# Two slots of edge attributes on one load of stationary columns, and digit tables made in fewer steps, in a graph network on one core

## What is computed

```python
def sage_conv(x, src, dst, W_l, b_l, W_r, n_nodes):
    agg = jax.ops.segment_sum(x[src], dst, num_segments=n_nodes)
    cnt = jax.ops.segment_sum(jnp.ones((src.shape[0], 1), x.dtype), dst, num_segments=n_nodes)
    return (agg / jnp.maximum(cnt, 1.0)) @ W_l.T + b_l + x @ W_r.T
def _mp_layer(x, src_f, dst_f, ea_f, W, b):
    m = jnp.concatenate([x[dst_f], x[src_f], ea_f], axis=1) @ W.T + b
    return jax.nn.relu(jax.ops.segment_sum(m, dst_f, num_segments=n))
x = _layernorm(x + _L0_gnn_ref(x, edge_index, ...), axis=-1)
x = _layernorm(x + _L1_gnn_ref(x, src, dst, edge_attr_16, ...), axis=-1)
```

## Time and profile before

| | us |
|---|---|
| median of 3 runs | 1181.01 (1178.44 to 1189.15) |
| the profiled execution | 1185.87 |
| its span from first to last instruction | 1184.0 |
| TensorE / VectorE / ScalarE busy over the span | 1054.0 / 711.7 / 368.8 |
| mean granted TensorE clock, share of full | 0.933 |

### The profile page before, as it was taken

One profiled execution on the slowest core, in us unless ns is written; L12 is line 12 of the kernel. 1 busy time (PEld: TensorE's weight loads), 2 busy tenths in 40 slices (PEclk: granted clock), 3 DMA queues, 4 the chain that ended last, 5 costly groups with the idle time before them and its releaser, 6 DMA issues. The chain is left out here.

```text
span 1184.0 us, 21105 instructions
## 1 busy us (share of the span) xinstructions
PE 1054.0 (89%) x8433; PEld 656.5 (55%) x8433; DVE 711.7 (60%) x1415; ACT 368.8 (31%) x733; POOL 104.9 (9%) x125
## 2 busy tenths in 40 slices
PE   0259999999999997999999999996899998899993
PEld 0258888899999984445555444443344444344441
DVE  5698979899899852623434755444555654233434
ACT  2475667686776530200000011113310105100000
POOL 4121212232211110000000000000000000000001
PEclk9968888899898897999999999998899998899997
DMA  6325535646455448963875436745036745037740
GB/s 160 48 69 196 187 112 204 201 135 234 126 173 170 120 171 254 404 257 127 311 277 219 164 118 267 290 150 218 14 122 240 289 179 218 18 122 270 287 181 22
DMA packets 67310, 216.89 MB, mean 183 GB/s; under 512 B 32176, under 2 KB 45227, under 8 KB 53667
## 3 DMA queue, kind: packets, MB, share of 16 engines
q1 hardware_dynamic: 59188, 164.51, 39.2%
q0 software_dynamic: 8016, 50.95, 12.0%
HBM read 170.68 MB, written 44.74 MB: 182 GB/s over the span
## 5 line engine op out<-in xcount | busy, mean ns | idle before, releaser
L1325 PE MATMUL PM<-Aring,Xop 128*128 128x512 fp8e4 (+1 forms) x1960 | 398.5, 363 | 0.0
L1325 PEld LDWEIGHTS PM<-Aring,Xop 128*128 128x128 f16 x1960 | 181.6, 98 | 216.6 <-issue 16.3
L1848 ACT ACTIVATE F<-PH,bag 64x512 f32<-64x512 f32 (+1 forms) x39 | 25.4, 657 | 382.4 <-PE PH L1544 382.3
L1325 PE MATMUL PM<-Ares,Xop 128*128 128x512 fp8e4 x588 | 137.0, 387 | 2.2 <-ACT Xop L1887 1.4
L772 PE MATMUL PW<-Aring 128*128 128x52 fp8e4 (+3 forms) x2151 | 115.9, 217 | 19.6 <-ACT F L836 17.6
L772 PEld LDWEIGHTS PW<-Aring 128*128 128x128 fp8e4 x2151 | 111.6, 103 | 22.8 <-ACT F L836 19.2
L785 PE MATMUL PA<-Ares,ea 128*128 128x32 f16 x1867 | 112.3, 235 | 0.0
L1681 DVE TENSOR_SCALAR S<-PM 128x256 f32<-128x256 f32 (+1 forms) x75 | 31.4, 418 | 130.6 <-PE PM L1325 118.8
L785 PEld LDWEIGHTS PA<-Ares,ea 128*128 128x128 f16 x1867 | 108.5, 116 | 0.0
L1325 PEld LDWEIGHTS PM<-Ares,Xop 128*128 128x128 f16 x588 | 55.9, 99 | 72.7 <-issue 10.0
L836 ACT ACTIVATE F<-PW 128x392 uint16<-128x392 f32 x196 | 85.4, 510 | 7.7 <-PE PW L772 5.4
(11 more groups left out here) (154 smaller groups left out, 1121.1 us busy)
## 6 DMA issues: line engine op xcount, KB each, us to landing
Aring<-adj SPq DMA_DIRECT2D x72, 1568.0 KB, 9.8
adj<-Aring POOLq DMA_DIRECT2D x12, 1568.0 KB, 6.1
adj<-Xop POOLq DMA_DIRECT2D x12, 1568.0 KB, 6.3
Ares<-adj SPq DMA_DIRECT2D x6, 1568.0 KB, 22.0
rc<-ea_sum SPq DMA_DIRECT2D x36, 128.0 KB, 5.8
eaf<-in_erow SPq DMA_DIRECT2D x62, 51.0 KB
Aring<-adj SPq DMA_DIRECT2D x4, 784.0 KB, 4.3
rc<-rc_d SPq DMA_DIRECT2D x12, 256.0 KB, 10.6
```

What stands on the lines that cost most here:

```text
L1325: last = nc.tensor.matmul(o, x[:, h, :], rhs, start=h == 0, stop=h == NT - 1)
L1848: nc.scalar.activation(F[0:64, c:c + w], PH[b % 2][0:64, 0:w], ACT.Relu, bias=t["bag"][:, 4 + conv:5 + conv]).then_inc(s_hr, 1)
```

## The change

- **Attribute slots in pairs.** The operand `ea16` is laid out in groups of two slots, 80 columns apart: slot 0 has columns 0 to 31, slot 1 columns 32 to 63, column 64 is the ones. `ohd` holds the two slots' one-hot columns interleaved. One matmul loads the columns of both slots and moves 64 columns for both, or 32 where only one of the two belongs to the window (`steps()` lists them). Of each product half is used; `sums` reads the even columns from partitions 0 to 31 and 64, the odd ones from 32 to 63 and 64, into `eas` and the new `odd`, with four copies for one; gpsimd adds the two before it stores the sum.
- **Low parts.** `eax` goes. ScalarE's `high(c)` is one copy; VectorE subtracts in place in `eaf` and raises `s_rest`; a new `low(c)` on ScalarE scales the remainder into `ea16` and raises `s_lo`. It stands behind `table` in ScalarE's round.
- **Digit tables.** `B` is made with its value in it by a bitwise and of patterns, in place of a comparison and a product (`valued`); the last value is half and doubled by a factor per partition in `evacuate` (`level`). `D` and its product become one scalar_tensor_tensor of 128 elements per value. `digits` has three more small tensor_tensor instructions.

```diff
@@ -164,9 +164,11 @@
 PD = 32
 NPW = NP // PD
+PJ[-1] += sum(PJ) % 2
+GW = 80
...
+def steps():
...
-        D = within(1, [128, 4, 128], u16)
-        Bv = within(2, [128, 8, 128], u16)
-        ohd = within(2, [128, 4, PD, CH], f16)
+        ohd = within(2, [128, 4, CH // 2, PD, 2], f16)
-        eax = sb("eax", [128, 2, CH, 16])
-        ea_flat = sb("ea16", [128, 4, CH * 33 + 95], f16)
-        ea16 = ea_flat[:, :, 0:CH * 33].rearrange("p g (k c) -> p g k c", c=33)
+        odd = sb("odd", [33, 2, SW])
+        ea_flat = sb("ea16", [128, 4, CH // 2 * GW + 48], f16)
+
+        def part(r, n, at):
+
+            x = ea_flat[:, r, 0:n // 2 * GW].rearrange("p (g k) -> p g k", k=GW)[:, :, 0:64]
+            return x.rearrange("p g (s c) -> p g s c", c=32)[:, :, :, at:at + 16]
...
@@ -535,6 +580,9 @@
                     for st in sums_after(h - 1):
                         n = SW if st < NST - 1 else LASTW
                         g.wait_ge(s_eas, st + 1)
+                        nc.gpsimd.tensor_tensor(eas[:, st % 2, 0:n], eas[:, st % 2, 0:n], odd[:, st % 2, 0:n],
+                                                ALU.add).then_inc(s_add, 1)
+                        g.wait_ge(s_add, st + 1)
                         g.dma_start(m["ea_sum"][:, st * SW:st * SW + n], eas[:, st % 2, 0:n]).then_inc(s_eo[st % 2], 16)
@@ -577,28 +625,29 @@
                 node, src, d = vs[:, t % 2, 0, :], vs[:, t % 2, 1, :], dig[:]
                 op = nc.vector.tensor_scalar
-                op(d[:, 1], src, 0x0E, None, ALU.bitwise_and)
+                op(d[:, 1], src, 4, 8, ALU.logical_shift_right, ALU.bitwise_and)
-                op(d[:, 5], node, 6, 0x40, ALU.logical_shift_left, ALU.bitwise_and)
-                op(d[:, 6], src, 3, 8, ALU.logical_shift_left, ALU.bitwise_and)
-                op(d[:, 7], src, 4, 8, ALU.logical_shift_right, ALU.bitwise_and).then_inc(s_dig, 1)
+                op(d[:, 5], src, 1, 7, ALU.logical_shift_right, ALU.bitwise_and)
+                op(d[:, 6], node, 6, 0x40, ALU.logical_shift_left, ALU.bitwise_and)
+                op(d[:, 7], src, 3, 8, ALU.logical_shift_left, ALU.bitwise_and).then_inc(s_dig, 1)
                 v.wait_ge(s_dig, 2 * t + 1)
-                tt = nc.vector.tensor_tensor
-                own(tt(d[:, 4:6], d[:, 4:6], base[:], ALU.bitwise_or))
-                tt(d[:, 4:6], d[:, 4:6], d[:, 6:8], ALU.logical_shift_left).then_inc(s_dig, 1)
-
-            def onehot(to, n, first_, table):
+                tt, u = nc.vector.tensor_tensor, d.bitcast(u16)
+                wait = tick(tt(d[:, 4], d[:, 4], d[:, 6], ALU.bitwise_or))
+                over = tick(tt(d[:, 5], d[:, 5], d[:, 7], ALU.bitwise_or))
+                v.wait_ge(s_own, wait)
+                own(tt(d[:, 4], d[:, 4], base[:, 0], ALU.bitwise_or))
+                v.wait_ge(s_own, over)
+                tt(u[:, 5], one[:], u[:, 5], ALU.logical_shift_left)
+                tt(u[:, 4], u[:, 4], u[:, 1], ALU.logical_shift_left).then_inc(s_dig, 1)
+
+            def onehot(to, n, first_, table, how=ALU.is_equal):
...
-                    table.rearrange("p (o g s) -> p o g s", o=1, s=16).broadcast_to(shape), ALU.is_equal)
-
-            def valued(to, of, n, table):
-                return nc.vector.tensor_tensor(
-                    to, of, table.bitcast(u16).rearrange("p (o s) -> p o s", o=1).broadcast_to([128, n, 128]), ALU.mult)
+                    table.rearrange("p (o g s) -> p o g s", o=1, s=16).broadcast_to(shape), how)
...
                 d, w = dig[:], wide(t)
-                onehot(B[:], 8, 8, d[:, 1])
-                wait = tick(onehot(D[:, 0:w], w, 42, d[:, 3]))
+                onehot(B[:].bitcast(i16), 8, 8, d[:, 5], ALU.bitwise_and)
                 onehot(A[:], 8, 0, d[:, 0])
+                for i in range(w):
+                    nc.vector.scalar_tensor_tensor(Dv[:, t % 2, i, :], d[:, 3], 4.0 * i, d[:, 4], ALU.is_equal, ALU.mult)
                 shape = [128, HS, 26, 2]
                 nc.vector.tensor_tensor(
                     H[:, t % 2], iv[:].rearrange("p v (o e) -> p o v e", o=1).broadcast_to(shape),
-                    d[:, 2].rearrange("p (q o e) -> p q o e", o=1, e=2).broadcast_to(shape), ALU.is_equal)
-                v.wait_ge(s_own, wait)
-                valued(Bv[:], B[:], 8, d[:, 4])
-                valued(Dv[:, t % 2, 0:w], D[:, 0:w], w, d[:, 5]).then_inc(s_sm, 1)
+                    d[:, 2].rearrange("p (q o e) -> p q o e", o=1, e=2).broadcast_to(shape),
+                    ALU.is_equal).then_inc(s_sm, 1)
@@ -662,17 +710,16 @@
                     v.wait_ge(s_pp, c - 3)
                 own(nc.vector.tensor_tensor(vd[:, c % 2, 0:n], eaf[:, c % 3, 0:n, 16].bitcast(i32),
                                             pb[:, c * CH:c * CH + n], ALU.subtract))
-                shape = [128, PD, CH // 2, 2]
+                shape = [128, CH // 2, PD, 2]
                 nc.vector.tensor_tensor(
-                    ohd[:, r].rearrange("p d (q e) -> p d q e", e=2),
-                    iop[:].rearrange("p d (o e) -> p d o e", o=1).broadcast_to(shape),
-                    vd[:, c % 2].rearrange("p (o q e) -> p o q e", o=1, e=2).broadcast_to(shape), ALU.is_equal)
+                    ohd[:, r], iop[:].rearrange("p d (o e) -> p o d e", o=1).broadcast_to(shape),
+                    vd[:, c % 2].rearrange("p (q o e) -> p q o e", o=1, e=2).broadcast_to(shape), ALU.is_equal)
                 v.wait_ge(s_hi, c + 1)
-                nc.vector.scalar_tensor_tensor(ea16[:, r, 0:n, 16:32], ea16[:, r, 0:n, 0:16], -LO, eax[:, c % 2, 0:n, :],
-                                               ALU.mult, ALU.add).then_inc(s_lo, 1)
-
-            nc.vector.memset(base[:, 0], 0x40)
-            nc.vector.memset(base[:, 1], 0x08)
+                x = eaf[:, c % 3, 0:n, 0:16].rearrange("p (g s) c -> p g s c", s=2)
+                nc.vector.tensor_tensor(x, x, part(r, n, 0), ALU.subtract).then_inc(s_rest, 1)
...
@@ -776,15 +823,13 @@
                     last.then_inc(s_pe, 1)
                 for c in CHUNKS[h]:
                     pe.wait_ge(s_lo, c + 1)
-                    n = min(CH, NPS - c * CH)
-                    for i in range(n):
-                        w, j = PSLOT[c * CH + i]
+                    for w, j, e, f, start, stop in STEPS[c]:
+                        st, o = w // 8, w % 8 * 2 * PD
+                        if start and w % 8 == 0 and st >= 2:
                             pe.wait_ge(s_eas, st - 1)
-                        last = nc.tensor.matmul(PA[st % 2][:, w % 8 * PD:w % 8 * PD + PD],
-                                                ea_flat[:, c % 4, i * 33:i * 33 + 128], ohd[:, c % 4, :, i],
-                                                start=j == 0, stop=j == PJ[w] - 1)
+                        last = nc.tensor.matmul(
+                            PA[st % 2][:, o:o + 2 * PD].rearrange("p (d e) -> p d e", e=2)[:, :, e:f],
+                            ea_flat[:, c % 4, j * GW:j * GW + 128], ohd[:, c % 4, j, :, e:f], start=start, stop=stop)
                     last.then_inc(s_pp, 1)
@@ -813,7 +858,8 @@
                 nc.scalar.copy(At[:, t % 2], A[:].rearrange("p i (s o) -> p s i o", o=1).broadcast_to([128, 128, 8, 2]))
-                nc.scalar.copy(Bt[:, t % 2], Bv[:].rearrange("p j s -> p s j")).then_inc(s_tr, 1)
+                nc.scalar.copy(Bt[:, t % 2, :, 0:7], B[:, 0:7].rearrange("p j s -> p s j"))
+                nc.scalar.activation(Bt[:, t % 2, :, 7], B[:, 7], ACT.Copy, scale=0.5).then_inc(s_tr, 1)
             def high(c):
                 n = min(CH, NPS - c * CH)
@@ -821,10 +867,14 @@
                 act.wait_ge(s_el[c % 3], LANDED[c])
                 if c >= 4:
                     act.wait_ge(s_pp, c - 3)
-                if c >= 2:
-                    act.wait_ge(s_lo, c - 1)
-                nc.scalar.copy(ea16[:, r, 0:n, 0:16], eaf[:, c % 3, 0:n, 0:16])
-                nc.scalar.mul(eax[:, c % 2, 0:n, :], eaf[:, c % 3, 0:n, 0:16], LO).then_inc(s_hi, 1)
+                nc.scalar.copy(part(r, n, 0),
+                               eaf[:, c % 3, 0:n, 0:16].rearrange("p (g s) c -> p g s c", s=2)).then_inc(s_hi, 1)
+
+            def low(c):
+                n = min(CH, NPS - c * CH)
+                act.wait_ge(s_rest, c + 1)
+                nc.scalar.mul(part(c % 4, n, 16), eaf[:, c % 3, 0:n, 0:16].rearrange("p (g s) c -> p g s c", s=2),
+                              LO).then_inc(s_lo, 1)
             def evacuate(g):
...
                 nc.scalar.activation(to, PW[g % RING][:, 0:416].rearrange("p (q h) -> p h q", h=52)[:, 0:NT], ACT.Copy,
-                                     scale=32.0).then_inc(s_wev, 1)
+                                     scale=level[:, 0:1]).then_inc(s_wev, 1)
             def sums(st):
                 n = SW if st < NST - 1 else LASTW
                 act.wait_ge(s_pp, pa_end[st] + 1)
                 if st >= 2:
                     act.wait_ge(s_eo[st % 2], 16 * (st // 2))
```

(68 more changed lines are left out.)

2 lines of the change are left out of this document (removed).

## The result

The changed kernel takes 1250.74 us (median of 4 runs, 1249.86 to 1252.53), the kernel before beside it 1182.45 (1178.44 to 1189.15). The ratio is 1.0573, with a 95% interval of 1.0522 to 1.0625: 68 us slower. The forecast was 1202, so the direction was right and the size was not; the time lies outside the range.

What follows compares the result with a forecast made beforehand. It took TensorE and VectorE to be full at once. Its terms 37 + 6 - 4 + 3 - 22 + 1 gave +21 us: 1202 as a median from 1181.0, with range 1160 to 1232.

Steps and rivals of the forecast that it cites:

- The moved step: Refill of eaf: ScalarE's later s_lo makes the load late and VectorE wait; stalls of 37 and 6 us.
- take 2.5: Load of eaf: landing time after issue taken as 2.5 us, between bounds of a small store (2.5) and a large one (6.3).
- the rival of the stores: Matrix stores delay each later load of eaf, landings of 4 to 5 us: 1222 us; chance 0.10.
- What it takes back: VectorE's 29 us of old waits in build go for the most part: 22 us off (10 to 29).
- +37 and +6: VectorE's stalls for late loads of second chunks: 37 us in odd rounds, 6 us for the other kind.
- I take 0.7 in nine later pairs, 6 us: Second kind of stall: the load after an odd round's low comes late for VectorE; 6 us (0 to 20).
- gpsimd: I take 3: The 25 gpsimd adds of 33x256 cost 3 us, up to 20 if each held VectorE for its whole length.
- VectorE -4: Changes to small and digits save VectorE 4 us over 15 pairs (-10 to +12).
- evacuate ... 0 to 0.1 us each, I take 0: ScalarE's evacuate with its factor from memory costs 0 to 0.1 us each, counted as 0.
- The rival of the clock: TensorE, idle several us each round, returns at half clock and stays full; 1202 to 1215 us; chance 0.08.
- The hidden load: Rival: the load of eaf lands within VectorE's room, so no stall comes; 1152 us; chance 0.17.
- the cancelled one: Rival: landings of 1.5 us, 23 us of stall against 22 to 29 back; 1178 us, no measurable change; chance 0.17.

Runs made afterwards that it cites:

- run 1: Kernel before, with only the refill signal of eaf raised later, by ScalarE where the change has low; 1223.87 us, ratio 1.0327.
- runs 2 and 3: The change with four buffers of eaf in place of three, 1189.13 us; the change with low right behind evacuate, ahead of across, 1187.26 us.
- run 4: The change with the 25 adds on VectorE instead of gpsimd, low left where it is; 1234.74 us, ratio 1.0435.
- run 6: The change with both low right behind evacuate and the adds on VectorE; 1177.24 us, ratio 0.9974 against the kernel before.
- run 5: Kernel before with the change's digit tables and its per-partition factor in evacuate, no shared columns or sums; 1188.16 us, ratio 1.0059.
- Run 8: Kernel before with the factor of evacuate read from memory (level filled with 32.0) in place of a constant; 1186.28 us, ratio 1.0044.
- run 7: The change with low early and adds on VectorE, but the old digit tables and constant factor; 1173.32 us, ratio 0.9930 against the kernel before.
- run 9: Kernel before with VectorE's remainder subtraction left out except for one slot of a chunk's 32; 1182.12 us, ratio 0.9977.

## Why the prediction was wrong, and where it was right

**The moved step.** Right in its mechanism: the signal now comes from the end of ScalarE's round, the load lands late, run 1 shows it by itself at 40 us and runs 2 and 3 take it out at 62 to 63. Even the loop's length was nearly right. "About 28 us a pair late in `build`, where it was 24.4" is measured as 29.3, and 24.2 before. The landing "take 2.5" was a median of 2.65 us from the last issue, though 4.4 to 7.5 in six of the 26 chunks looked at; in each of the six a store of the matrix was issued within 3 us of that load, so the rival of the stores may have a small share; but six others had a store as near and took 1.8 to 3.2. One sign of being right failed: VectorE's waits in odd rounds do not grow with the number of DMAs. They are 0.8 to 2.6 us each from round 9 on, for 3 DMAs as for 7. In a closed loop a single wait doesn't show how late the load is, for the lateness of one turn has moved the next already. What was wrong is what became of the mechanism in the sum. Its three large terms all failed, and in one direction: the stalls by 14 us, what is taken back by 11, gpsimd's adds by 17.

**"What it takes back", 22.** This is the step where the reasoning failed. A loop that sets the time isn't shortened by waits that lie outside it. The forecast added stalls (37 + 6) and then took off waits that would vanish, as if they were room; a loop of 29.3 us against 24.2 is 5 us a pair, and from that nothing is to be subtracted. In VectorE's own books the old waits went from 31.4 to 20.4 us (without the end; the forecast counted 29.0, leaving out 2.4 for line 653), so 11 came back and not 22.

**"+37 and +6", by kinds.** VectorE's waits for the load and for `high` are 45.4 and 11.5 us from 80 us on, 56.9 in place of 43. The first kind, in odd rounds, is 23.8 us and was forecast at 37. The second, "I take 0.7 in nine later pairs, 6 us", is the mis-sized one: in even rounds VectorE waits 21.6 us. From `high` to the end of `low` was put at 6.5 us in odd rounds and is 7.1, and the load at 5.5 and is 6.2. The 11.5 us for `high` stood in no term of the sum. And the time up to round 9, whose chunks have one to three DMAs each and for which some 5 us were forecast, is 14 us longer. The loop has no term that is small when n is small: two trips of ScalarE (18.3 us of the 29.2) are in it whatever the load.

**"gpsimd: I take 3", bounds 0 to 20.** It was at the top: some 20 us of VectorE's time, 16 us of the run's in the change (run 4), 8 to 10 without the loop (run 6 against 3). The rule quoted in the forecast from the Trainium skill, "SBUF — State Buffer", section "SBUF: two separate sides", was right and should have had the weight: the comparisons and masks of 128x1024, which have two inputs, went from 684 to 1131 ns in the mean. Beyond what the forecast quoted, an add of 0.74 us stretched a VectorE instruction with one input from 0.18 to 1.22 us.

**"VectorE -4".** Right: without the stops VectorE's busy time in `build` is 366.9 us (376.8 less 9.9) against 370.0, -3.1. One scalar_tensor_tensor of 128x128 takes 280 ns, not the 200 taken, and three or four of them give back most of what `valued` cost. Busy time was saved, and run time wasn't (run 5).

**"evacuate ... 0 to 0.1 us each, I take 0".** 89 ns each, 196 times, 17 us of ScalarE's. The forecast gives no reason for nothing. Run 8 prices it at 4 to 5 us in the kernel before, though ScalarE was busy only 242 of 360 us; TensorE's column loads wait 22.2 us for the eviction there in place of 19.2.

**The sum again**, from what VectorE did in `build`: busy +17.2 (387.2 against 370.0), waits for the load +56.9, old waits -11.0, the longest one at the end 16.7 against 13.4, +3.3. That is 66.4 of the 68.3 by which `build` is longer; the rest lies in short gaps and ahead of 80 us. The forecast had -1, +43, -22, +1.

**TensorE and the clock.** The relief is real, and nearly the 50 us that were forecast: the trace has the 1001 matmuls of `PA`, busy 64.1 us in place of 112.3. From 60 to 420 us TensorE was busy 338.0 us before and 270.1 in run 7, which was ahead of it by then. It turns into 8 us of time, since VectorE, at 326 of 360 before, is at 331. The forecast put the relief off the path "where VectorE is full"; run 9 shows that TensorE held the kernel before, with VectorE close behind. The rival of the clock has its sign right (0.94 to 0.83 in the full stretch, and 0.69 from 60 to 120 us), but it follows from the loop: with the loop open (runs 2 and 3) the same arithmetic is granted 0.89.

**The rivals.** The hidden load and the cancelled one fall with the waits for `eaf`. The range was too narrow by the forecast's own terms: with nothing taken back and gpsimd's term at its top they give 37 + 6 - 4 + 20 + 1 = 60, a median of 1241, which stood in no rival. Even that is 10 us under the measured time.

## What to carry to other kernels

When a release signal moves to another engine, write down the whole loop it closes (signal, load, first use, the queue up to the next signal) and compare its length with the period, not with the slack of one wait; if it is longer, the difference is paid in every turn and old idle time pays none of it. A signal that frees a buffer belongs ahead of the long instructions of its engine: two lines moved were worth 63 us here. Small helper work isn't free on an engine with a low busy share: 25 adds on gpsimd cost 8 to 16 us through VectorE, and 0.09 us in each of 196 evictions costs 4 to 5 us where a ring of banks waits for them.

## What the runs showed of the hardware

- A gpsimd add of 33x256 elements in float32 takes 805 ns in the mean (0.74 in the row shown) and holds even a VectorE instruction with one input of 128x128 elements (1.22 us in place of 0.18); the 25 adds took some 20 us from VectorE. VectorE does the same add in 411 ns.
- An activation of 128x392 from a bank takes 510 ns with a constant factor and 595 to 599 with one from a column of memory (run 8 and the change).
- Stationary columns reused for twice the moving columns cost nothing more here: 32 matmuls of 64 columns in 1.92 us, 64 of 32 columns in 3.85.
